# A ring of five heads of probabilities, and a new order of projections, in a layer-norm, attention and expert kernel

## The reference

```python
xn = _layernorm(x, axis=-1)
s = _L0_attn_ref(xn, L0_attn_Wqkv, L0_attn_b_qkv, L0_attn_Wout, L0_attn_b_out)
g = _silu(_L0_ffn_ref(xn, L0_ffn_w_router, L0_ffn_w_fc, L0_ffn_w_proj))
x = x + s * g
# attention, for each of 16 heads:
scores = jnp.einsum('bqhd,bkhd->bhqk', q, k) * scale
scores = scores + bias[None, :, None, :]
scores = jnp.where(causal[None, None, :, :], scores, jnp.asarray(-1000000000.0, dtype=x.dtype))
p = jax.nn.softmax(scores, axis=-1)
ctx = jnp.einsum('bhqk,bkhd->bqhd', p, v).reshape(B, S, D)
return ctx @ Wout.T + b_out
```

## Time and profile before

| | us |
|---|---|
| median of 3 runs | 1522.3 (1521.74 to 1522.56) |
| the profiled execution | 1519.17 |
| its span | 1517.3 |
| PE busy in the span | 1393.7 (92%) |
| VectorE, ScalarE, GpSimd busy | 927.6, 770.8, 685.9 |
| PE waits for GpSimd's norms (`psT` for `pr`) | 19.2 in 17 |
| PE waits for masks (`psS` for `mn`) | 18.9 in 47 |

### The profile page before, as it was taken

The page is one execution under the profiler, slowest core; times in us unless marked ns, Lnnn a source line. Parts: engine busy times, 40 slices in busy tenths (PEclk is TensorE's granted clock), DMA queues, the critical chain, the costliest instruction groups (busy, mean ns, idle before and its releaser), DMA issues. The chain is left out here.

```text
span 1517.3 us, 30037 instructions
## 1 busy us (share of the span) xinstructions
PE 1393.7 (92%) x9860; PEld 883.8 (58%) x9860; DVE 927.6 (61%) x2438; ACT 770.8 (51%) x1824; POOL 685.9 (45%) x897
## 2 busy tenths in 40 slices
PE   2879999999999999999739999999999999999995
PEld 1455555655556565555426666666666666666663
DVE  7577677777776777766539954444455554444443
ACT  3477777786878777687616522222222222222221
POOL 0455657465555746556414443233333333233332
PEclk9999999999999999999969999999999999999998
DMA  4425334342533434243147511001111110101100
GB/s 157 147 77 159 108 102 150 112 127 86 165 98 104 147 112 129 85 136 109 39 135 242 189 42 35 24 29 43 43 42 41 37 43 29 29 29 43 35 29 29
DMA packets 84898, 133.45 MB, mean 88 GB/s; under 512 B 14096, under 2 KB 63248, under 8 KB 82577
## 3 DMA queue, kind: packets, MB, share of 16 engines
q1 hardware_dynamic: 75808, 105.70, 22.3%
q0 software_dynamic: 8944, 25.83, 5.4%
HBM read 97.81 MB, written 33.95 MB: 87 GB/s over the span
## 5 line engine op out<-in xcount | busy, mean ns | idle before, releaser
L1038 PE MATMUL psF<-xT,wf 128*128 128x256 f16 (+1 forms) x3264 | 370.4, 270 | 6.7 <-DVE wf L1141 6.7
L1056 PE MATMUL psY<-wf,aT 128*128 x1584 | 363.9, 379 | 0.3 <-DVE aT L1167 0.3
L1038 PEld LDWEIGHTS psF<-xT,wf 128*128 x3264 | 313.0, 98 | 71.8 <-issue 7.4
L1245 POOL TENSOR_TENSOR a<-a 128x512 f32<-128x512 f32 (+1 forms) x136 | 154.3, 1134 | 395.9 <-DVE a L1158 394.3
L880 POOL TENSOR_SCALAR pr<-pr,rden 128x128 f32<-128x128 f32 (+3 forms) x512 | 269.1, 545 | 135.9 <-DVE rden L796 134.6
L556 ACT ACTIVATE pr<-pr,mn 128x128 f32<-128x128 f32 (+3 forms) x512 | 281.9, 553 | 0.0
L785 DVE CUSTOM_DVE_ANT_0 pr<-psS,base,nsl 128x128 f32<-128x128 f32 (+3 forms) x512 | 249.9, 543 | 3.3 <-PE psS L412 2.9
L1056 PEld LDWEIGHTS psY<-wf,aT 128*128 128x128 f16 x1584 | 154.5, 98 | 158.5 <-issue 1.0
L433 PE MATMUL psT<-conf,pr 128*128 128x128 f32 x1280 | 208.3, 281 | 23.0 <-POOL pr L880 19.2
L433 PEld LDWEIGHTS psT<-conf,pr 128*128 128x128 f32 x1280 | 158.9, 144 | 88.9 <-POOL pr L880 27.6
L339 PE MATMUL psA<-xT,wqkv 128*128 128x512 f16 x768 | 195.3, 393 | 15.6 <-DVE wqkv L638 13.1
(11 more groups left out here) (149 smaller groups left out, 1371.1 us busy)
## 6 DMA issues: line engine op xcount, KB each, us to landing
qk_parts<-pre SPq DMA_DIRECT2D x64, 256.0 KB, 2.2
qs<-qk_parts SPq DMA_DIRECT2D x128, 128.0 KB, 2.7
ks<-qk_parts SPq DMA_DIRECT2D x128, 128.0 KB, 2.7
wst<-in_wf SPq DMA_DIRECT2D x16, 1024.0 KB, 5.6
wstage<-in_wf SPq DMA_DIRECT2D x32, 512.0 KB, 4.7
xin<-in_x SPq DMA_DIRECT2D x32, 256.0 KB, 4.0
attn_out<-so SPq DMA_DIRECT2D x32, 256.0 KB, 2.0
pt<-in_wqkv SPq DMA_DIRECT2D x4, 768.0 KB, 10.0
```

Source lines behind the costliest of these rows:

```text
L1038: last = nc.tensor.matmul(psF[c % 2][:, k * TT:k * TT + tn], w(e, 2 * hc, hl, kc * 512 + col, P), xT[:, r % 2, x, kc, 0:tn], start=(m == 0 ...
L1056: last = nc.tensor.matmul(psY[r % 2][h][:], aT[:, c % 4, x, k, h * P:(h + 1) * P], w(e, 2 * hc + 1, hl, q * 512, 512), start=(c == 0 and k ...
L1245: nc.gpsimd.tensor_tensor(at, at, at, ALU.mult).then_inc(s["a_ready"], 1)
```

## The change

Three things. The buffers of probabilities become a ring of five (`RP`), counted over batches. Scores, masks and exponentials each go one head further ahead (5, 4 and 3), and the reciprocal gets a lead of its own, `R_LEAD` = 2, and moves from the start of VectorE's step to its end; GpSimd keeps `N_LEAD` = 1. And `JOBS` and `STEP` are new: most jobs move up one step. q(0,2) of the batch becomes q(1,2) in step 15 of the batch before, the k, q, k that follow stand in steps 0, 1 and 2, the four pairs of o and x in steps 3 to 6 instead of 4 to 7, q and k of the next batch's group 0 in steps 7 and 8 instead of 8 and 9, of its group 1 in 11 and 12 instead of 12 and 13; v in 9, 10, 13, 14. The positions of ctx stay in steps 0, 4, 8 and 12. The cast and low part `cx` of group 3 move from step 2 to step 1. In the first iteration the weights are prepared in step 7 instead of 8. `WMAX_AT`, `ln_stats`, `ln_apply` and SP's list stay.

```diff
--- before.py
+++ after.py
@@ -100,19 +100,19 @@
 
 
 WEIGHTS = ["q", "k", "logits", "v", "o"]
-JOBS = [("q", 0, 2), ("ctx", -1, 3), ("k", 0, 2), ("q", 0, 3), ("k", 0, 3),
-        ("o", -1, 0), ("x", 1, 0), ("ctx", 0, 0), ("o", -1, 1), ("x", 1, 1),
-        ("x", 1, 2), ("o", -1, 2), ("o", -1, 3), ("x", 1, 3),
-        ("q", 1, 0), ("ctx", 0, 1), ("k", 1, 0), ("logits", 1, 0), ("v", 1, 0),
-        ("v", 1, 1), ("q", 1, 1), ("ctx", 0, 2), ("k", 1, 1), ("rank", 1, 0),
-        ("v", 1, 2), ("v", 1, 3)]
-STEP = [(0, 1), (2,), (3,), (4,), (5, 6, 7), (8, 9), (10, 11), (12, 13),
+JOBS = [("k", 0, 2), ("ctx", -1, 3), ("q", 0, 3), ("k", 0, 3), ("o", -1, 0), ("x", 1, 0),
+        ("o", -1, 1), ("x", 1, 1), ("ctx", 0, 0), ("o", -1, 2), ("x", 1, 2),
+        ("o", -1, 3), ("x", 1, 3), ("q", 1, 0), ("k", 1, 0), ("ctx", 0, 1), ("v", 1, 0),
+        ("logits", 1, 0), ("v", 1, 1), ("q", 1, 1), ("k", 1, 1), ("ctx", 0, 2), ("v", 1, 2), ("rank", 1, 0),
+        ("v", 1, 3), ("q", 1, 2)]
+STEP = [(0, 1), (2,), (3,), (4, 5), (6, 7, 8), (9, 10), (11, 12), (13,),
         (14, 15), (16,), (17, 18), (19,), (20, 21), (22, 23), (24,), (25,)]
 WMAX_AT = (5, 8, 12, 14)
 NJOB = len(JOBS)
 ABANKS = 2
 
-S_LEAD, M_LEAD, E_LEAD, N_LEAD = 4, 3, 2, 1
+RP = 5
+S_LEAD, M_LEAD, E_LEAD, R_LEAD, N_LEAD = 5, 4, 3, 2, 1
 
 
 def job_exists(b, pos):
@@ -164,10 +164,10 @@
         qs = sb("qs", [P, 2, HG, S], F16)
         ks = sb("ks", [P, 2, HG, S], F16)
         v = sb("v", [P, 2, QB, D], F32)
-        pr = sb("pr", [P, HG, CAUSAL], F32)
-        mn = sb("mn", [P, HG * QB], F32)
-        den = sb("den", [P, HG * QB], F32)
-        rden = sb("rden", [P, HG * QB], F32)
+        pr = sb("pr", [P, RP, CAUSAL], F32)
+        mn = sb("mn", [P, RP * QB], F32)
+        den = sb("den", [P, RP * QB], F32)
+        rden = sb("rden", [P, RP * QB], F32)
         pt = sb("pt", [P, 2, HG, CAUSAL], F32)
         cf = sb("cf", [P, S], F32)
         cx = sb("cx", [P, NG, 2, S], F16)
...
@@ -547,12 +547,12 @@
 
                         if not within(hb, 0, B):
                             return
-                        c = (h % HG) * QB + i
+                        c = ((hb * H + h) % RP) * QB + i
                         if i == 0:
 
-                            wait(act, s["rden_done"], hb * H + h - HG + 1)
+                            wait(act, s["rden_done"], hb * H + h - RP + 1)
                         wait(act, s["ttr_done"], (hb * H + h) * QB + i + 1)
-                        p_ = pr[:, h % HG, ROWOFF[i]:ROWOFF[i] + (i + 1) * P]
+                        p_ = pr[:, (hb * H + h) % RP, ROWOFF[i]:ROWOFF[i] + (i + 1) * P]
                         nc.scalar.activation(p_, p_, ACT.Exp, bias=mn[:, c:c + 1], scale=-1.0,
                                              accum_out=den[:, c:c + 1]).then_inc(s["exp_done"], 1)
 
...
@@ -611,7 +611,7 @@
                     largest(3, wr_f[:, :])
                 if step == 5:
                     largest(2, wo_f, (s["w_in"], 16))
-                for kc in {6: (0,), 7: (1,), 8: (2, 3)}.get(step, ()):
+                for kc in {5: (0,), 6: (1,), 7: (2, 3)}.get(step, ()):
                     largest(4 + kc, wq_f[:, kc * 3 * D:(kc + 1) * 3 * D], (wq_in[kc], 16))
 
             def prepare():
...
@@ -777,23 +777,16 @@
                         if not within(hb, 0, B):
                             return
                         if i == 0:
-                            wait(dve, s["T_done"], (hb * H + h - HG + 1) * 3)
+                            wait(dve, s["T_done"], (hb * H + h - RP + 1) * 3)
                         w = (i + 1) * P
-                        c = (h % HG) * QB + i
+                        c = ((hb * H + h) % RP) * QB + i
 
                         wait(dve, s["S_done"], (hb * H + h) * QB + max(i, 1) + 1, s["apart_dve"])
                         nc.vector.tensor_tensor_reduce(
-                            out=pr[:, h % HG, ROWOFF[i]:ROWOFF[i] + w], in0=rows[i],
+                            out=pr[:, (hb * H + h) % RP, ROWOFF[i]:ROWOFF[i] + w], in0=rows[i],
                             in1=base[:, S - w:S], scale=nsl[:, h:h + 1], scalar=3e38,
                             op0=ALU.add, op1=ALU.min, accum_out=mn[:, c:c + 1]).then_inc(s["ttr_done"], 1)
 
-                    rb, rh = head_at(b, step + N_LEAD)
-                    if within(rb, 0, B):
-
-                        wait(dve, s["exp_done"], (rb * H + rh + 1) * QB)
-                        wait(dve, s["norm_done"], (rb * H + rh - HG + 1) * QB)
-                        c = (rh % HG) * QB
-                        nc.vector.reciprocal(rden[:, c:c + QB], den[:, c:c + QB]).then_inc(s["rden_done"], 1)
                     masked(0)
                     masked(1)
                     masked(2)
...
@@ -818,13 +811,20 @@
                         nc.vector.tensor_tensor(fam[:, c:c + 1], fam[:, c:c + 1], fam[:, 2:3], ALU.max
                                                 ).then_inc(s["wm_link"], 1)
                         dve.wait_ge(s["wm_link"], b * 4 + m + 1)
-                    if j == (3 if g else 2):
+                    if j == (3 if g else 1):
 
                         pb, pg = (b, g - 1) if g else (b - 1, NG - 1)
                         if within(pb, 0, B):
                             wait(dve, s["ctx_staged"], pb * NG + pg + 1)
                             wait(dve, s["O_done"], pb * QB + 1)
                             nc.vector.tensor_copy(cx[:, pg, 0, :], cf[:]).then_inc(s["ctx_hi"], 1)
+                    rb, rh = head_at(b, step + R_LEAD)
+                    if within(rb, 0, B):
+
+                        wait(dve, s["exp_done"], (rb * H + rh + 1) * QB)
+                        wait(dve, s["norm_done"], (rb * H + rh - RP + 1) * QB)
+                        c = ((rb * H + rh) % RP) * QB
+                        nc.vector.reciprocal(rden[:, c:c + QB], den[:, c:c + QB]).then_inc(s["rden_done"], 1)
                 assert not more or k[0] == LINKS, k[0]
 
             batches(dve, iteration)
...
@@ -875,8 +875,8 @@
 
                         wait(pool, s["rden_done"], rb * H + rh + 1, s["apart_pool"])
                         for i in range(QB):
-                            c = (rh % HG) * QB + i
-                            p_ = pr[:, rh % HG, ROWOFF[i]:ROWOFF[i] + (i + 1) * P]
+                            c = ((rb * H + rh) % RP) * QB + i
+                            p_ = pr[:, (rb * H + rh) % RP, ROWOFF[i]:ROWOFF[i] + (i + 1) * P]
                             nc.gpsimd.tensor_scalar(p_, p_, rden[:, c:c + 1], 32768.0, ALU.mult, ALU.mult
                                                     ).then_inc(s["norm_done"], 1)
                     for kind, bj, i, _, _ in jobs(b, odd, step, ("q", "k")):
...
@@ -895,7 +895,7 @@
                         nc.gpsimd.tensor_tensor(rstd[:, par, :], veps[:], half[:], ALU.pow
                                                 ).then_inc(s["rstd_ready"], 1)
                     pb, pg = (b, g - 1) if g else (b - 1, NG - 1)
-                    if j == (3 if g else 2) and within(pb, 0, B):
+                    if j == (3 if g else 1) and within(pb, 0, B):
                         wait(pool, s["ctx_hi"], pb * NG + pg + 1, s["apart_pool"])
                         nc.gpsimd.tensor_tensor(cx[:, pg, 1, :], cf[:], cx[:, pg, 0, :], ALU.subtract
                                                 ).then_inc(s["ctx_lo"], 1)
```

More of the change, by code:

```diff
@@ L432, in ptrans @@
                         c = ROWOFF[i] + kb * P
-                        last = nc.tensor.transpose(ps[:, o:o + P], pr[:, j, c:c + P],
+                        last = nc.tensor.transpose(ps[:, o:o + P], pr[:, h % RP, c:c + P],
                                                    conf[:, C_ID:C_ID + P])
@@ L527, in iteration @@
                     g, j = step // HG, step % HG
-                    if isinstance(b, int) and b == -1 and step == 8:
+                    if isinstance(b, int) and b == -1 and step == 7:
                         prepare()
@@ L756, in iteration @@
                         magnitudes(step)
-                        if step == 8:
+                        if step == 7:
                             prepare()
```

## The result

| | before | after |
|---|---|---|
| median of the runs, us | 1522.43 (4) | 1539.98 (4) |
| the profiled execution | 1519.17 | 1540.07 |
| its span | 1517.3 | 1538.2 |

The changed kernel takes 1.0133 times as long, 95% interval 1.0118 to 1.0148 (the two medians by themselves give 1.0115). Medians differ by 17.6, the two profiled executions by 20.9; the forecast was +33.0 on the latter basis, a median of 1555 in the range 1532 to 1574. Direction and outer range held. The fourth run of the changed kernel took 1546.77, with a granted clock of 0.972 over the span where the others had 0.975 to 0.977. So one kernel's time can differ by 7 us between executions, along with the clock, and what follows counts the falls of one execution.

A forecast was written before the change was run, and what follows sets the result against it. PE was 9 tenths busy, so only its own waits and clock falls counted. Terms 7.0 + 3.4 + 1.0 + 14.1 + 7.5 = 33.0 took 1519.2 to 1552.2, median 1555; own range 1545 to 1568, outer 1532 to 1574.

The forecast's parts named there:

- step 1: Before step 1, `pre` of q(1,2) delays `cx` on GpSimd: new PE wait of 1.1 us (0.6 to 1.5).
- step 3: Before step 3, `cx` of group 3 on GpSimd delays head 3's norms: PE wait longer by 0.9 us (0.7 to 1.2).
- step 14: In step 14, `place` begins 1.0 us earlier, shortening PE's waits: -1.0 us per batch (-1.15 to 0).
- `xT`: At step 7, q(1,0) waits 0.7 us for `xT` instead of 0.22: +3.4 us in seven batches (0 to 5).
- batch boundary: Steps 14, 1 and 3 together: +1.0 us per boundary, +7.0 us over seven (1 to 12).
- late casts: VectorE's casts in steps 7 and 11 delay masks by at most 0.15 us: +1.0 us in all (0 to 2).
- stack at step 11: Step 11's scores need `ks` before its DMA lands, behind load `wst`: seven waits of 1.4 to 3.5, +14.1 us (10 to 18).
- clock: New waits at step 11 bring four clock falls of 1.67 us, plus half a fall elsewhere: +7.5 us (0 to 13).
- The start and the end: One job and one head's scores move from batch 0 to the start; last batch's chain unchanged: 0 us (-3 to 2).
- rival A: Stack not late at step 11, so its 14.1 us and falls go and 12.2 stay: 1535 us; chance 0.14.
- Value 0 for ring and lead: Fifth buffer and longer leads: 0 us (bound -17.0); VectorE's removed waits for ScalarE precede none of PE's listed waits.
- rival C: Older exponentials let head 3's norms begin early, removing step 3's wait: 29 us saved, 1493 us; chance 0.08.

The follow-up runs named there:

- old leads: Kernel before with the new table, its `cx` place and weight preparation, keeping the ring of four and former leads: 1529.5 us, ratio 1.0045.
- stack first: Changed kernel with SP's second weight-maximum load issued behind the stack of the next batch's group 0: 1530.2 us, ratio 1.0050.
- e11: Changed kernel with q(.,2) taken back from step 15 to step 0, ahead of k(.,2): 1565.9 us, ratio 1.0272.
- scatters' kernel: Changed kernel with all four indirect stores in step 14 instead of two each in steps 14 and 15: 1559.4 us, ratio 1.0247.
- layer norm first: Changed kernel with reciprocal behind masks, norms two heads ahead, stack before weight load, x(1,3) before o(-1,3), layer norm before read-outs: 1481.8 us, ratio 0.9738.

## Why the prediction was right, and where it was not

I put the six inner periods together from the batch without a fall of the kernel before, 86.77, and the new waits. Per batch: step 1 +1.20, step 3 +0.55, step 14 -1.15, `xT` +0.15, in all 0.75. The waits of step 11 in these six sum to 10.04. 6 × (86.77 + 0.75) + 10.04 = 535.2; measured 541.7, so falls cost 6.5. Before it was 528.85 - 6 × 86.77 = 8.2. Step 0 of batch 1 begins 8.2 later than before (158.10 against 149.92). Of that, 2.0 is the first wait for the stack and an estimated 3.1 is moved work: two products of 1.3 and a head's scores of 0.5, which the last batch no longer has. The remaining 3.1 is the start; behind the six periods the same 3.1 makes -0.1 into 3.0. This gives the 20.9 of the spans:

| term | predicted | measured |
|---|---|---|
| batch boundary and `xT`, late casts | 7.0 + 3.4 + 1.0 | 4.5 |
| stack at step 11, seven waits | 14.1 | 12.0 |
| clock | 7.5 | -1.7 |
| start | 0 | 3.1 |
| last batch and end of attention | 0 | 3.0 |
| sum | 33.0 | 20.9 |

The split between the first row and the clock is good to about 1.5: the three batches without a fall, less their wait for the stack, took 87.3, 87.6 and 87.3. By 87.3 the first row is 3 and the falls cost 8, as they did before.

- **The mechanisms of the waits** were right. The lead of five asks for the stack too early (old leads and stack first each take the wait away), and `pre` of q(1,2) on GpSimd makes the wait of step 1 (`e11`), with 1.20 for 1.1. The seven waits for the stack were 12.0 for 14.1.
- **The batch boundary and `xT`** came out at less than half, 4.5 for 11.4, of which 1.2 belongs to the last batch and stands in its row. Step 3 got 0.55 for 0.9: the norms took 2.28 at 445.96 where they took 2.70, more than I credited. `xT` waits 0.39 for 0.7. The late casts exist (22 of them took 1.27 or 1.28 us beside GpSimd's `pre`), but no wait of PE at steps 7 and 11 shows them.
- **The step that failed is the clock**, "four falls of 1.67 in seven, and half a fall for the one batch that had none": +7.5, measured -1.7 to 0. I had made the fall a price of a wait, rising with its length. It isn't one: one and the same wait of 2.35 brought a fall in six of six with old leads and with the stack first, and in three of six in the changed kernel; a wait of 3.01 brought none in three of seven batches of the scatters' kernel. Of the seven new waits at step 11 one had a fall, the longest (2.57); the six of 1.19 to 1.98 had none. And step 3 fell in three inner batches where it had fallen in five. The Trainium skill (TensorE: Matmul & The Clock Gate, HAM oscillation) tells of a kernel whose clock fell at each repeated DMA wait. I had read that as all seven falling, and that is not borne out here; its waits were longer than the matmuls between them, and here nearly a whole busy batch lies between two. What chooses isn't settled: with the same waits in every batch and none at step 11, old leads and stack first fall in six of six, but the kernel before in five of six; the kernels that also wait at step 11 fall irregularly. Once the waits of step 3 are gone, no inner batch falls.
- **The start and the end** were set to 0 and cost 6. The start lost 3.1 beside its wait for the stack; 0.8 of it is PE's first wait for `ks` (4.5 instead of 3.7), and the rest I can't name. At the end stand the new wait of 1.20 before step 1 of the last batch, two waits of 0.85 for the banks, which the parity of the o jobs would have given, and a first o product of 4.24 us, at a clock of 0.72 in the 6 us from there.
- **Luck** has a part in the total. The clock was 9.2 too high, the boundary 6.9, the stack 2.1, and the start and end 6.1 too low, which hides a third of the error. The nearest number on record was rival A's 1535, whose condition (a stack that is not late) did not come true.
- **Value 0 for ring and lead** was right for masks, exponentials and norms, and only with the norms one head ahead. "So the effect is that of the new table" was wrong: the table by itself costs 7.8, and the term of the stack, which I counted, belongs to the lead of five. With the stack in time, the lead of five alone changes nothing (1.0050 against 1.0045), since the norms stay where they were. My rival C saw this room ("older exponentials let the norms of head 3 begin early") and gave it 29 us; it fell as I wrote, because GpSimd works in order. With the norms moved, the room is there: 33 us for one edit.

## What to carry to other kernels

In this kernel a deeper buffer and a longer lead gave nothing by themselves: the operation that PE waits for had to move up in its own engine's order too. Judge an order table only with that done, since here the same table was 8 us worse on one side of the edit and 9 us better on the other. When a consumer asks a step earlier, follow the load back through its whole DMA queue, and look for a big transfer in front that nobody needs soon.

## What the runs showed of the hardware

- A store of 256 KB landed in 2.2 us alone and in 5.6 behind a load of 1 MB issued 0.4 before it in the same queue.
- VectorE's cast of 128x512 took 0.41 to 0.43 us with GpSimd idle (kernel before), 1.27 or 1.28 in all 22 places where it met GpSimd's `pre` (changed kernel), and 0.39 to 1.45 beside the norms alone (layer norm first). The longest, beside both, took 3.28.
- An indirect store occupied GpSimd for 0.95 to 1.31 us, with some 0.30 between two, so 1.26 from one to the next.
- A clock fall cost 1.66 us a batch (88.43 against 86.77), a deep one about 2.9 (the batch of 178.00: 91.56, less its 1.40 for the stack, against 87.3). Whether a wait brings one can't be read from its length alone: 1.81 and 2.35 did and didn't, and 3.01 didn't in three of seven.
